# Counting edges by node from the given destinations, two blocks earlier in a graph transformer kernel

## What is computed

```
h = jnp.maximum(_layernorm(x, axis=-1), 0.0)
# gt_layer, twice:
a = (kw * q_i).sum(-1) * pri[:, etype].T / SQRT_D
alpha = ex / (den[dst] + 1e-16)                       # softmax over the edges of one dst
agg = jax.ops.segment_sum(alpha[..., None] * m, dst, num_segments=n)
```

## Time and profile before

| | |
|---|---|
| median of three runs | 2824.23 us |
| the profiled execution's own time | 2824.39 us |
| its span | 2822.7 us |
| busy share PE / DVE / ACT / POOL | 67 / 76 / 54 / 70% |
| mean granted TensorE clock | 0.772 |
| block `edge_tables`, first and last start on the trace | 50.65 to 182.52 us |

### The profile page before, as it was taken

How to read it: one execution, slowest core, us unless ns; L and a number is a source line. 1 busy time by engine, 2 the same in 40 slices (tenths; PEclk the granted TensorE clock), 3 DMA queues, 4 the chain that set the end, 5 groups by cost and what they waited for, 6 DMA issues and landing times. The chain is left out here.

```text
span 2822.7 us, 53679 instructions
## 1 busy us (share of the span) xinstructions
PE 1902.4 (67%) x12612; PEld 1692.1 (60%) x12612; DVE 2146.3 (76%) x5513; ACT 1519.7 (54%) x5159; POOL 1971.6 (70%) x2072
## 2 busy tenths in 40 slices
PE   1877747766777767776577747777777767667466
PEld 1755536666666666666455546666666666666344
DVE  6977758777777777777577757777777777777587
ACT  0027625555555555555577725555555555555555
POOL 3716667777777777777277777777777777777176
PEclk8569968777787787777688967778778787787655
DMA  5528876666666666665266776666666666665411
GB/s 135 88 109 346 342 204 186 185 184 183 186 184 184 185 184 185 185 185 169 68 244 276 292 203 184 184 184 183 184 185 183 183 184 184 183 184 163 116 45 37
DMA packets 396315, 512.23 MB, mean 181 GB/s; under 512 B 75449, under 2 KB 311419, under 8 KB 383508
## 3 DMA queue, kind: packets, MB, share of 16 engines
q0 software_dynamic: 102144, 327.28, 37.3%
q1 hardware_dynamic: 284760, 179.79, 21.8%
q10 hardware_dynamic: 9104, 1.86, 0.4%
HBM read 383.54 MB, written 142.96 MB: 187 GB/s over the span
## 5 line engine op out<-in xcount | busy, mean ns | idle before, releaser
L1243 POOL DMA_INDIRECT g_rows<-node_kv,g_ids x1568 | 1485.0, 947 | 474.8 <-issue 444.2
L1499 PE MATMUL g_ps_q<-g_qw,g_hot_t 128*128 128x128 f32 x3136 | 593.7, 357 | 61.8 <-DMA g_qw<-node_q 50.0
L1419 ACT ACTIVATE acc<-acc,g_gained,g_scale x1568 | 600.9, 383 | 3.0 <-issue 2.1
L1499 PEld LDWEIGHTS g_ps_q<-g_qw,g_hot_t 128*128 128x128 f32 x3136 | 546.6, 265 | 71.2 <-DMA g_qw<-node_q 51.6
L1415 ACT ACTIVATE acc<-g_ps_sum 128x127 f32 x1568 | 411.5, 262 | 317.5 <-DVE g_gained L1348 257.3
L1480 PE MATMUL g_ps_sum<-g_hot,g_rows 128*128 128x128 f32 x3136 | 553.6, 331 | 5.9 <-ACT acc L1419 5.7
L1480 PEld LDWEIGHTS g_ps_sum<-g_hot,g_rows 128*128 128x128 f32 x3136 | 512.0, 245 | 12.5 <-ACT acc L1419 8.4
L1270 DVE TENSOR_TENSOR g_rows<-g_rows,g_ps_q 128x512 f32<-128x512 f32 x448 | 274.5, 613 | 317.4 <-DMA g_rows<-node_kv,g_ids 290.0
L1488 PE MATMUL g_ps_hot<-ident,g_hot_t 128*128 128x128 f32 x1568 | 293.3, 312 | 18.2 <-ACT g_hot L1424 17.9
L1424 ACT ACTIVATE g_hot<-g_ps_hot 128x512 f32<-128x512 f32 x448 | 233.2, 521 | 56.1 <-PE g_ps_hot L1488 56.1
L1488 PEld LDWEIGHTS g_ps_hot<-ident,g_hot_t 128*128 128x128 f32 x1568 | 230.2, 169 | 28.0 <-ACT g_hot L1424 25.1
(11 more groups left out here) (243 smaller groups left out, 3265.1 us busy)
## 6 DMA issues: line engine op xcount, KB each, us to landing
g_qw<-node_q SPq DMA_DIRECT2D x1568, 64.0 KB
g_rank_row<-edge_rank SPq DMA_DIRECT2D x112, 448.0 KB
g_rows<-node_kv,g_ids POOLq DMA_INDIRECT x1568
node_agg<-n_agg SPq DMA_DIRECT2D x24, 256.0 KB, 3.1
node_rows<-node_x SPq DMA_DIRECT2D x2, 1792.0 KB
node_q<-l_blank_q SPq DMA_DIRECT2D x1, 3200.0 KB
node_q<-n_q_sb,node_slot POOLq DMA_INDIRECT x112
node_kv<-n_kv,node_id POOLq DMA_INDIRECT x112
```

The lines of the kernel that those rows point to most:

```text
L1243: g_.indirect_dma_start(out=rows[b % U][:, g, :], out_offset=None, in_=scratch["kv"][:, :], in_offset=bass.IndirectOffsetOnAxis(ap=ids[b / ...
L1419: a.activation(at, at, ACT.Identity, scale=scale[b % 2][:, 0, g:g + 1], bias=gained[q % 2][:, n:n + 1]).then_inc(s["joined"], 1)
L1499: ins = t.matmul(ps_q[q % 2][:, n, :], hot_t[b % 2][:, g, :], qw[b % 2][:, g, :], start=True, stop=True)
```

## The change

The count no longer uses the sorted and padded list, transposed on chip. It uses the destinations as they were given, loaded once more in `edge_lists` as 128 partitions x 781 with the 32 left over in a column of their own (a count does not depend on the order of the edges). `edge_lists` makes `dst_lo` and `dst_hi` from them. In `edge_tables` the one-hot tables of four batches are made ahead of the wait for `cur`, `prev` and `key`, two more behind `cid`, then come ranks, flags and keys, and then the other 50 batches. TensorE counts four batches, does the sum over partitions and the 7 transposes of the keys, and counts the rest. The transposes and copies of `lo` and `hi` go, ScalarE's among them.

```
 edge_lists, SyncE, behind the loads of L177 and L178
+    sp.wait_ge(s["pads"], 1)
+    sp.dma_start(dst_all[:, 0:ALL], dst[0:P * ALL].rearrange("(p w) -> p w", w=ALL)).then_inc(s["all_in"], 16)
+    with nc.allow_non_contiguous_dma(reason="a few words, once"):
+        sp.dma_start(dst_all[0:E - P * ALL, ALL:ALL + 1], dst[P * ALL:E].rearrange("(p w) -> p w", w=1)).then_inc(s["all_in"], 16)
     sp.wait_ge(s["loaded"], 144)
 edge_lists, VectorE
     v.memset(lead[:, :], -1).then_inc(s["filled"], 1)
+    v.memset(dst_all[:, ALL:T], N).then_inc(s["pads"], 1)
...
     v.sem_inc(s["ready"], 1)
+    dve.wait_ge(s["all_in"], 32)
+    then(v.tensor_scalar(dst_part[:, :], dst_all[:, :], P - 1, None, ALU.bitwise_and))
+    then(v.tensor_copy(tab["dst_lo"][:, :], dst_part[:, :]))
+    then(v.tensor_scalar(dst_part[:, :], dst_all[:, :], 7, None, ALU.arith_shift_right))
+    then(v.tensor_copy(tab["dst_hi"][:, :], dst_part[:, :]))
     dve.wait_ge(s["prev_in"], 16)
 edge_tables, SyncE, ahead of the stores of L502 to L506
-    sp.wait_ge(s["dv"], 12)
+    sp.wait_ge(s["dv"], 9)
 edge_tables, VectorE
+    then(v.tensor_copy(row_of[:, :, :], c["row"][:, :].rearrange("p (r o) -> p r o", o=1).to_broadcast([P, P, G])))
+    for b in range(AHEAD):
+        hots(b, b % 2, b >= 2)
     dve.wait_ge(s["loaded"], 48)
     did(v.tensor_tensor(start[:, :], cur[:, :], prev[:, :], ALU.not_equal))
-    did(v.tensor_copy(keyf[:, :], key[:, :]))
-    did(v.tensor_scalar(lo_i[:, :], cur[:, :], P - 1, None, ALU.bitwise_and))
-    then(v.tensor_scalar(hi_i[:, :], cur[:, :], 7, None, ALU.arith_shift_right))
-    did(v.tensor_copy(lo[:, :], lo_i[:, :]))
-    did(v.tensor_copy(hi[:, :], hi_i[:, :]))
+    then(v.tensor_copy(keyf[:, :], key[:, :]))
     then(v.tensor_tensor_scan(cid[:, :], start[:, :], start[:, :], 0.0, ALU.add, ALU.max))
+    for b in range(AHEAD, AHEAD + BESIDE):
+        hots(b, b % 2)
     dve.wait_ge(s["pe"], 1)
...
-    then(v.tensor_copy(row_of[:, :, :], c["row"][:, :].rearrange("p (r o) -> p r o", o=1).to_broadcast([P, P, G])))
     dve.wait_ge(s["pe"], 2)
-    did(v.tensor_copy(tiles_of(tab["key"][:, 0:T]), ps_t[0][:, 0:K7, 0:Q]))
-    dve.wait_ge(s["pe"], 4)
-    then(v.tensor_copy(tiles_of(hi_t[:, :]), ps_t[0][:, 0:K7, 0:Q]))
-    dve.wait_ge(s["lows"], 1)
-    hots(0, 0, None)
-    hots(1, 1, None)
-    with dve.Fori(1, HALF) as i:
+    did(v.tensor_copy(tiles_of(tab["key"][:, 0:T]), ps_t[:, 0:K7, 0:Q]))
+    with dve.Fori((AHEAD + BESIDE) // 2, HALF) as i:
 edge_tables, ScalarE
-    act.wait_ge(s["pe"], 3)
-    nc.scalar.activation(tiles_of(lo_t[:, :]), ps_t[1][:, 0:K7, 0:Q], ACT.Copy).then_inc(s["lows"], 1)
 edge_tables, TensorE
-    pe.wait_ge(s["dv"], 7)
-    t.matmul(ps_s[0:Q, 0:1], c["before"][0:Q, 0:Q], cid[:, W - 1:W], start=True, stop=True).then_inc(s["pe"], 1)
-    (7 transposes each of keyf, lo and hi)
     pe.wait_ge(s["filled"], 1)
     t.matmul(ps_h[:, :], zero_b[:, :], zero_b[:, 0:NT], start=True, stop=False)
+    for b in range(AHEAD):
+        count(b, b % 2)
+    pe.wait_ge(s["dv"], 4)
+    t.matmul(ps_s[0:Q, 0:1], c["before"][0:Q, 0:Q], cid[:, W - 1:W], start=True, stop=True).then_inc(s["pe"], 1)
+    for k in range(K7):
+        last = t.transpose(ps_t[:, k, 0:Q], keyf[:, k * P:(k + 1) * P], c["ident"][0:Q, 0:Q])
+    last.then_inc(s["pe"], 1)
-    with pe.Fori(0, HALF) as i:
+    with pe.Fori(AHEAD // 2, HALF) as i:
```

More of the change, by code:

```diff
@@ L164, in edge_lists @@
         blank_q = sb("l_blank_q", [P, 1, D])
+        ALL = E // P
+        dst_all, dst_part = sb("l_dst_all", [P, T], I32), sb("l_dst_part", [P, T], I32)
         ps, ps_kind, ps_before, ps_all, ps_id = pb("l_ps", [1, 1]), pb("l_ps_kind", [P, 512]), pb("l_ps_before", [P, 512]), pb("l_ps_all", [P, 512]), pb("l_ps_id", [P, 512])
@@ L465, in edge_tables @@
         sb = lambda n, sh, d=F32: st.enter_context(nc.sbuf_tensor(n, sh, d))
-        cur, prev, key, lo_i, hi_i = (sb(f"e_{n}", [Q, W], I32) for n in ("cur", "prev", "key", "lo_i", "hi_i"))
-        start, cid, rank, keyf, lo, hi = (tab["h"][0:Q, k * K7:(k + 1) * K7, :].rearrange("p t d -> p (t d)") for k in range(6))
+        cur, prev, key = (sb(f"e_{n}", [Q, W], I32) for n in ("cur", "prev", "key"))
+        start, cid, rank, keyf = (tab["h"][0:Q, k * K7:(k + 1) * K7, :].rearrange("p t d -> p (t d)") for k in range(4))
         base, w0 = sb("e_base", [Q, 1]), sb("e_w0", [Q, K7])
@@ L470, in edge_tables @@
         new_f, pas_f = sb("e_new", [Q, K7], BF16), sb("e_pas", [Q, K7], BF16)
-        lo_t, hi_t = sb("e_lo_t", [P, T], BF16), sb("e_hi_t", [P, T], BF16)
         row_of = sb("e_row_of", [P, P, G], BF16)
@@ L483, in edge_tables @@
         slot_f = sb("e_slot_f", [P, TT])
-        ps_t = [st.enter_context(nc.psum_tensor(f"e_ps_t{u}", [P, K7 + 1, P], F32)) for u in range(2)]
+        ps_t = st.enter_context(nc.psum_tensor("e_ps_t", [P, K7 + 1, P], F32))
         ps_h = st.enter_context(nc.psum_tensor("e_ps_h", [P, NT], F32))
@@ L491, in edge_tables @@
         HALF = B // 2
+        AHEAD, BESIDE = 4, 2
         tiles_of = lambda a: a.rearrange("p (q k) -> p k q", k=K7)
@@ L537, in then, with hots @@
                     dve.wait_ge(s["dv"], n[0])
+                def hots(b, u, waits=True):
+                    if waits:
+                        dve.wait_ge(s["counted"], b - 1)
+                    v.tensor_tensor(hot_lo[u][:, :, :], row_of[:, :, :],
+                                    tab["dst_lo"][:, bass.ds(b * G, G)].rearrange("p (o g) -> p o g", o=1).to_broadcast([P, P, G]),
+                                    ALU.is_equal).then_inc(s["hot"], 1)
+                    v.tensor_tensor(hot_hi[u][:, :, :], row_of[:, 0:NT, :],
+                                    tab["dst_hi"][:, bass.ds(b * G, G)].rearrange("p (o g) -> p o g", o=1).to_broadcast([P, NT, G]),
+                                    ALU.is_equal).then_inc(s["hot"], 1)
+                then(v.tensor_copy(row_of[:, :, :], c["row"][:, :].rearrange("p (r o) -> p r o", o=1).to_broadcast([P, P, G])))
+                for b in range(AHEAD):
+                    hots(b, b % 2, b >= 2)
                 dve.wait_ge(s["loaded"], 48)
                 did(v.tensor_tensor(start[:, :], cur[:, :], prev[:, :], ALU.not_equal))
-                did(v.tensor_copy(keyf[:, :], key[:, :]))
-                did(v.tensor_scalar(lo_i[:, :], cur[:, :], P - 1, None, ALU.bitwise_and))
-                then(v.tensor_scalar(hi_i[:, :], cur[:, :], 7, None, ALU.arith_shift_right))
-                did(v.tensor_copy(lo[:, :], lo_i[:, :]))
-                did(v.tensor_copy(hi[:, :], hi_i[:, :]))
+                then(v.tensor_copy(keyf[:, :], key[:, :]))
                 then(v.tensor_tensor_scan(cid[:, :], start[:, :], start[:, :], 0.0, ALU.add, ALU.max))
+                for b in range(AHEAD, AHEAD + BESIDE):
+                    hots(b, b % 2)
                 dve.wait_ge(s["pe"], 1)
@@ L559, in _ @@
                                            op0=ALU.mult, op1=ALU.add))
-                then(v.tensor_copy(row_of[:, :, :], c["row"][:, :].rearrange("p (r o) -> p r o", o=1).to_broadcast([P, P, G])))
                 dve.wait_ge(s["pe"], 2)
-                did(v.tensor_copy(tiles_of(tab["key"][:, 0:T]), ps_t[0][:, 0:K7, 0:Q]))
-                dve.wait_ge(s["pe"], 4)
-                then(v.tensor_copy(tiles_of(hi_t[:, :]), ps_t[0][:, 0:K7, 0:Q]))
-                dve.wait_ge(s["lows"], 1)
[L568 to L576, removed]
-                hots(0, 0, None)
-                hots(1, 1, None)
-                with dve.Fori(1, HALF) as i:
-                    hots(i * 2, 0, i)
-                    hots(i * 2 + 1, 1, i)
+                did(v.tensor_copy(tiles_of(tab["key"][:, 0:T]), ps_t[:, 0:K7, 0:Q]))
+                with dve.Fori((AHEAD + BESIDE) // 2, HALF) as i:
+                    hots(i * 2, 0)
+                    hots(i * 2 + 1, 1)
                 dve.wait_ge(s["counted"], B + 1)
@@ L586, in _ @@
                 did(v.tensor_copy(num[:, :], n_i[:, :]))
-                dve.wait_ge(s["pe"], 5)
+                dve.wait_ge(s["pe"], 3)
                 did(v.tensor_copy(pre[:, :], ps_s[:, 64:64 + NT]))
@@ L610, in _ @@
                 did(v.tensor_copy(tab["slot"][:, :], slot_f[:, :]))
-            @block.scalar
-            def _(act):
-                act.wait_ge(s["pe"], 3)
-                nc.scalar.activation(tiles_of(lo_t[:, :]), ps_t[1][:, 0:K7, 0:Q], ACT.Copy).then_inc(s["lows"], 1)
             @block.tensor
@@ L639, in _ @@
                 t.matmul(ps_h[:, :], zero_b[:, :], zero_b[:, 0:NT], start=False, stop=True).then_inc(s["counted"], 1)
-                pe.wait_ge(s["dv"], 16)
+                pe.wait_ge(s["dv"], 11)
                 t.matmul(ps_s[:, 64:64 + NT], c["before"][:, :], has[:, :], start=True, stop=True)
@@ L1572, in gnn @@
         tab["at_place"] = places.enter_context(nc.sbuf_tensor("at_place", [P, NT, P], BF16))
+        tab["dst_lo"] = places.enter_context(nc.sbuf_tensor("dst_lo", [P, T], BF16))
```

(1 more changed line is left out.)

2 lines of the change are left out of this document (1 added, 1 removed).

## The result

The changed kernel takes **2807.58 us** in the median of four runs (2805.68 to 2809.07), the kernel before 2824.69 (2822.65 to 2826.42): a ratio of 0.9939, interval 0.9922 to 0.9957, faster by 17 us. The forecast was 2811.7, range 2808.3 to 2816.3. The interval of the ratio stands for 12 to 22 us, so it still holds the 12.5 us of the forecast. The profiled execution of the changed kernel, 2805.68 us, is the fastest of its four, so the two profiles differ by more than the medians do.

What follows compares the result with a forecast made beforehand. GpSimd issuing edge-stage gathers was the largest row, left alone; VectorE and TensorE set the end of `edge_tables`. 14.8 us gained there less 2.3 in `edge_lists` gave 12.5 us, so 2811.7 us by the median, range 2808.3 to 2816.3.

Steps and rivals of the forecast that it cites:

- The block: `edge_tables`, from its start to the first table of batch 6: 18.4 us instead of 33.2, a gain of 14.8 us.
- The four batches ahead: Start of `edge_tables`: four batches made before the loads are needed take 6.3 us and hide the loads with 1.3 to spare.
- `edge_lists`: Four new VectorE operations of 128 x 784 on its own path cost 2.3 us, between 2.1 and 3.4.
- L217's delay: `edge_lists`: the two new loads could delay L217 by up to 1.5 us; taken as 0, later than 12.7 a sign against.
- The pace of the count: Count in `edge_tables`: a pair of batches takes 3.28 us before and after, at a clock of 0.50.
- The loop of two engines: Count: VectorE's tables 1.59 us until TensorE starts, then 1.70 until the buffer is released, 3.29 in all, set the pace.
- On everything behind the block I put nothing: Node stage and later: no gain or loss counted, since the node stage waits only for the block.
- the clock at the start of the node stage: First node stage: its clock changes won't fall on the same work, a little over 1 us in the range.
- the spread of executions: Whole kernel: three executions spread by 1.3 us either way, a term of the range.
- First rival, the count at 2.4 GHz: Count in `edge_tables`: at full clock a pair takes 2.88 us instead of 3.28, 10 us more gained, 2801.7; chance 0.05.
- Second rival, the gathers: `edge_tables`: slowed GpSimd gathers end the block if their pace exceeds 1.93 us; at 2.40, 2837 us; chance 0.02 for slower.
- the forecast's dearest row: `edge_tables`: the `node_x` gather beginning at 61.68, beside VectorE's scan, took 2.10 us instead of 1.14 to 1.25.

Runs made afterwards that it cites:

- r4: The changed kernel with AHEAD = BESIDE = 0, so no batches counted ahead or beside: 2816.92 us, 0.9977 of the kernel before.
- r1: The changed kernel once more, unaltered: 2809.05 us (five runs) against 2823.25 for the kernel before, ratio 0.9945.
- r2: The kernel before once more, unaltered: ratio 0.9997.
- r11: The changed kernel with three buffers for the one-hot tables instead of two: 0.9963 of the kernel before, in a group where that takes 3520 to 3526 us.
- r8: The changed kernel with three unread filler matmuls (128x512) behind each batch's 14: 1.0031 of the kernel before, in a group where that takes 3520 to 3526 us.
- r12: The kernel of r8 with count matmuls reading neighbouring elements instead of every 14th; output not the reference's, one run, whose time says nothing.
- r18: The changed kernel with unread filler matmuls, 28 ahead of TensorE's wait for the slot tables and 16 first in the node stage: 2805.5 us, 0.9938 of the kernel before.
- r16: The kernel of r11 again, three table buffers: 0.9979 of the kernel before, in a group where that takes 3520 to 3526 us.
- r17: The kernel of r4 again, nothing made ahead or beside: 2816.67 us, 0.9975 of the kernel before.

## Why the prediction was right, and where it was wrong

*The block: right.* 14.8 us were forecast between the block's start and batch 6, measured 33.2 - 17.96 = 15.2. The four batches ahead took 60.87 - 54.81 = 6.06 (forecast 6.3), rank and flags 2.75 (2.75), the two batches beside 2.88 (2.9), the keys 1.38 (1.6). The loads were hidden, as was the sum over partitions. r4 shows their price without the cover: 5.87 us of waiting in one place and a node stage that starts 7 to 8 us later.

*`edge_lists`: right.* 2.42 us for the four operations (2.3). L217's delay, taken at 0 with 1.5 as its end, was 0.6 in the first profile (13.24, later than the 12.7 that the forecast had named as a sign against it), and nearly nothing in r1 (12.70 against 12.62 and 12.75). In sum the node stage starts 12.2 us earlier in the first profiles (12.5 forecast), and 13.4 between r1 and r2: there the delay is missing, and r2's loads landed 0.45 us later than those of the first profile, which only the kernel before pays.

*The pace of the count: right, its reason in part.* 3.28 us a pair stayed to the hundredth. The loop of two engines is what sets it, as r11 shows by breaking it. What the forecast took for the price of the 14 matmuls at 1.2 GHz is the price of their stride (r8, r12).

*The step that failed* is "On everything behind the block I put nothing", with "a little over 1 us" in the range for the clock at the start of the node stage, and 1.3 us for the spread of executions. The first node stage alone took from 174.2 to 180.0 us over eight executions, with 0 to 13.7 of its first 20 us at the lower clock; in the first two profiles it was 5.8 us shorter after the change. And the spread was read from three runs; the 25 beside r1 go from 2819.99 to 2827.61. The path to the node stage was right to 0.3 us in the first pair of profiles and to 0.9 in the second. The range around it was too narrow by the stage behind. With 3 us either way for that stage in place of a little over 1, it would have held the time. Nor do its own terms give its lower end: 1.3 and a little over 1, with 0.2 for cheaper operations, are 2.6 us, and it lies 3.4 below the forecast.

Chance has a large part in the miss: the five runs of r1, the same kernel, have their median at 2809.05, inside the range.

*What stays open:* whether the stage is shorter in the changed kernel on average. The medians give 17.1 and 14.2 us, the block 12.2 and 13.4. r18 limits what the clock could give: with the full clock until 2.8 us from its end the stage still takes 174.6. Two profiles of each kernel can't separate a shift of 2 us from chance.

*First rival, the count at 2.4 GHz:* did not happen, and its price was wrong too. It said that at the full clock the loop would be shorter. r8 had the clock and kept 1.49 us for 14 matmuls. By the Trainium skill, page "TensorE: Matmul & The Clock Gate", section "Part 1: The HAM clock gate", activity releases the throttle. The changed kernel's trace disagrees, as that of the one before did: its count ran at 0.50 from the first batch to the last. In r8, with three fillers a batch, the clock did rise.

*Second rival, the gathers:* did not happen. The last gather ended at 148.8 and SyncE's store was issued at 149.94, 20 us before the block's end. The pace was 1.68 us from start to start, against 1.93 at which the gathers would have set the end. But gathers do wait for VectorE, by far more than the forecast's dearest row, and that took r11 and r16 down. In the changed kernel its trace is the gather of 3.46 us at 71.93, beside the tables of batches 6 and 7, from 71.58 to 74.52, in which VectorE has no pause.

## What to carry to other kernels

A wait for loads is worth as much work as is ready without them: find a form of the input that is already there (here the unsorted, unpadded list, since a count has no order), and the wait, the transposes and the copies go together. Where GpSimd issues indirect transfers beside VectorE, they may need VectorE's idle tenths of a microsecond, and a buffer that removes those can cost tens (45 us here). And before a range is drawn around a saving of 0.5%, the stage behind it should be given the spread that several executions show, not that of three medians.

## What the runs showed of the hardware

- Matmuls with weights and moving data 28 bytes apart (128x128 and 128x50, bf16) take 106 ns each at a granted clock of 0.50 (rows 3) and of 1.00 (r8, 1.49 us for 14); with neighbouring elements 55 ns at 0.50 and 38 ns at 1.00 (r12, 0.77 and 0.53 us for 14).
- An indirect DMA on GpSimd waited 72.39 us behind one-hot tables of VectorE (`tensor_tensor`, bf16) that followed each other without a gap (r11; 72.38 in r16).
- The same kernel takes 2823 us in some groups of runs and 3520 in others, one chip number stands beside both, and the gain of one change is 14 to 17 us there and 54 here.
- Ahead of the first change of clock that a trace shows, the rows say 1.00 even where the work does not: L289's 50 matmuls took 4.73 us before, while the slot matmuls of the same shape took 2.63 in r18 at 1.00 and 4.85 in r17 at 0.50.
